# A two-layer GRU with a mixture of experts on one core: r's sums by a copy, ACT mixture work behind the tanh of n, a shorter preamble

## Chip, cores and metric

The kernel runs on one core of a Trainium2 chip, in fp32. The metric is the device time of one execution in microseconds (us). PE is the matrix engine, DVE the vector engine, ACT the scalar engine, POOL the GpSimd engine; SP issues the DMAs. Instructions of an engine run in the order of its program; engines wait for each other by semaphores.

## The reference, cut to what matters

```python
# x: [2, 1024, 256]; context: [2, 256]
mixed = tanh(x @ W_in.T + b_in + context)
h1 = gru(mixed, Wih0, Whh0, bih0, bhh0)
h2 = gru(h1, Wih1, Whh1, bih1, bhh1)
gate = sigmoid(context @ W_gate.T + b_gate)
x = x + (gate * h2 + h2) @ W_out.T + b_out
shared = silu(x @ w1) * (x @ w3) @ w2
s = sigmoid(concat(x, context) @ router_W)          # 8 experts, the best 2 by s + router_bias
routed = sum over experts e of combine[:, e] * (gelu(x @ W1e[e]) @ W2e[e])
out = x + (shared + routed) / 3

# one step of a GRU
r = sigmoid(xr + hr); z = sigmoid(xz + hz)          # x* = x @ Wih.T + bih, h* = h @ Whh.T + bhh
n = tanh(xn + r * hn)
h = (1 - z) * n + z * h
```

## The kernel before, in words

The two GRU layers run interleaved. A slot s holds step s of layer 0 and step s - LAG of layer 1 (`schedule`, L263); LAG is 20. There are 1024 steps, in chunks of CH = 16; j is the place in a layer-0 chunk, s % 16. Time steps and the two sequences of the batch lie along PSUM partitions: a chunk has 32 rows, four strips of 32 partitions hold four quarters of the 256 units.

PSUM holds, for each layer and each of two chunks in turn, `sums` (four parts of 64 columns: the state's part of n, then z, r, and the input's part of n) and `r_sums` (r alone). Ahead of a chunk they are filled with biases and with the product of the chunk's inputs and w_x. The input product is made in pieces on PE (`projection_pieces`, L52, `project_at`, L344): piece R (`project_r`, L308, 64 columns into `r_sums`) and pieces A, one for each half kt of the inputs (`project_all`, L313, 192 columns into `sums`). Layer 0's pieces stand at j = 8, 10 and 12 behind layer 1's products of the slot, layer 1's at j = 1, 2 and 3 ahead of them. Biases for the chunk after next come by two ACT copies, r's at a chunk's step 1 (L472), all at step 2 (L484).

A step of a layer, in the order of its dependences:

- PE: state times w_h for r (L330, 64 columns, into `r_sums`), then for n and z (L340, 128 columns). At j = 6 and 14 (`r_first`) one product of 192 columns makes all three, and r is turned later.
- DVE: r turned by 32x32 transposes (L402), then n (L411) and z (L412).
- ACT: tanh for r (L470) and for z (L478).
- DVE: a scan makes xn + r * hn (L420); ACT: tanh of n (L482); POOL: half the old state (L520).
- DVE: a scan makes the new state (L431).

At j = 13, and for layer 1 at j = 3, DVE turns the input's part of n of the next chunk (`turn_xn`, L387), layer 0's between the scan of n and the state scan, layer 1's behind the scan of n and so ahead of layer 0's turn of r and layer 1's state scan of the next slot (`dve_slots`, L434). POOL copies the chunk's inputs to `stage` at j = 0 (L525, L550), and SP clears the semaphores of the chunk before last.

Beside this runs the rest, for groups of 128 steps (256 rows), one group MLAG = BODY + LAG + 5 slots behind. The class `Mixture` (L64) makes its plan once: each operation gets a half slot (0: beside layer 0's step, 1: beside layer 1's), an engine does one a half slot, and `busy` (L92) names half slots that stay free. An ACT or DVE operation may stand in the same half slot as the PE product that it reads. A group has 94 products on PE, 83 operations on DVE and 22 on ACT: the tanh of 2 score halves (L656), the tanh of 4 shared units (L677), the gelu of 8 experts in 2 halves each (L688). In `act_slots` (L493) the first half slot's operation stands between layer 0's tanh of r and its tanh of z and n; the second one's between layer 1's tanh of r and of z and n.

The first product of the kernel, tanh(x @ W_in.T + ...), is made in blocks of TB = 512 rows. Ahead of the first slot PE makes the gate's products, the router's from the context, the first block, the biases of both layers in 128-row products against ones, and the first chunk's input product; the other blocks follow in pieces (`MIXING`) between slots 4 and 31.

The order within a slot on PE and the places of the ACT and DVE mixture work:

```python
recur(pe, 0, t0)                       # then MIXING piece, layer 1's input piece
mixture_at(pe, "pe", s, 0, base)
recur(pe, 1, t1)                       # then layer 0's input piece
```

## Time and profile before

| | |
|---|---|
| median of 3 runs | 2235.19 us (2231.73 to 2236.82) |
| profiled execution | 2234.58 us |
| its span (first to last instruction) | 2232.8 us |
| mean granted share of PE's clock | 0.995 |
| busy: PE, DVE, ACT, POOL | 94%, 82%, 53%, 24% |

In a row, "a<-b" is what is written and read by the program's names, "x16" the number of instructions merged (an fp32 product is two instructions; eight products of four strips are x16), and the bracket is the engine's idle time just before and what ended it. L431 is a line of the kernel. A busy PE means that a product is in flight, its fill included.

### The profile page before, as it was taken

The numbers are of one execution on the slowest core, as the hardware profiler recorded it, in microseconds if no ns is written. First come the engines' busy times: TensorE is split into PE (matmuls) and PEld (weight loads), VectorE is DVE, ScalarE is ACT, GpSimd is POOL, SyncE is SP. The second block draws the span as 40 slices with busy tenths as digits, with TensorE's granted clock in tenths as the row PEclk, the third lists the DMA queues.
The fourth block names the chain that finished last, engine by engine and source line by source line (L and its number), as shares of the span: only waits on it lengthen the run. The fifth ranks groups of instructions, "written<-read, shape, count | busy, mean of one in ns | idle before, by whom it ended". The sixth has DMA issues, their size and how long they took to land.

```text
span 2232.8 us, 165488 instructions
## 1 busy us (share of the span) xinstructions
PE 2095.5 (94%) x71788; PEld 1526.4 (68%) x71788; DVE 1835.4 (82%) x11070; ACT 1193.2 (53%) x6589; POOL 541.5 (24%) x2410
## 2 busy tenths in 40 slices
PE   6989899999999999999999999999999999999968
PEld 4666666677776776777767677777777677677744
DVE  4788888888888888888888888888888888888853
ACT  2555555555555555555555555555555555555531
POOL 1222222222222222222222222222222222222210
PEclk9999999999999999999999999999999999999998
DMA  5000000000000000000000000000000000000000
GB/s 214 4 5 5 5 5 5 23 5 5 10 5 24 5 5 9 5 24 5 5 10 24 5 5 10 5 24 5 5 10 5 24 5 5 9 5 24 5 8 26
DMA packets 7772, 32.98 MB, mean 15 GB/s; under 512 B 1328, under 2 KB 3456, under 8 KB 5760
## 3 DMA queue, kind: packets, MB, share of 16 engines
q1 hardware_dynamic: 7040, 22.38, 2.7%
q8 instruction: 562, 9.21, 1.6%
q14 instruction: 170, 1.39, 0.2%
HBM read 20.22 MB, written 2.16 MB: 10 GB/s over the span
## 4 chain that ended last, share of the span: by engine, by line
PE 56%; DVE 27%; ACT 13%; issue 3%; DMA 1%; SPq 0%; POOL 0%; DVEq 0%; POOLq 0%
PE bank L340 24%; PE bank L330 19%; PE bank L273 10%; DVE n_first L411 9%; DVE cells L431 8%; ACT factors L478 6%; ACT cells L482 5%; DVE r_pre L402 4%; DVE z_pre L412 3%; PE bank L313 3%; DVE bank L420 1%; PE bank L308 1%; ACT act_t L688 1%; ACT act_t L677 0%; PE bank L636 0%
## 5 line engine op out<-in xcount | busy, mean ns | idle before, releaser
L340 PE MATMUL bank<-w_h,cells 128*14 128x128 f32 (+4 forms) x32768 | 1362.7, 281 | 18.3 <-DVE cells L431 10.9
L340 PEld LDWEIGHTS bank<-w_h,cells 128*14 128x14 f32 (+4 forms) x32768 | 857.5, 110 | 118.5 <-DVE cells L431 85.1
L330 PEld LDWEIGHTS bank<-w_h,cells 128*14 128x14 f32 (+4 forms) x28672 | 533.1, 112 | 528.9 <-DVE cells L431 501.8
L330 PE MATMUL bank<-w_h,cells 128*14 128x64 f32 (+4 forms) x28672 | 787.4, 224 | 97.1 <-DVE cells L431 79.2
L520 POOL TENSOR_SCALAR cells<-cells 128x4 f32<-128x4 f32 x2048 | 463.6, 226 | 1615.4 <-DVE cells L431 1612.5
L470 ACT ACTIVATE n_second<-r_pre 128x4 f32<-128x4 f32 x2048 | 426.3, 208 | 538.3 <-DVE r_pre L402 509.9
L478 ACT ACTIVATE factors<-z_pre 128x4 f32<-128x4 f32 x2048 | 428.2, 209 | 403.6 <-DVE z_pre L412 345.0
L431 DVE TENSOR_TENSOR_SCAN cells<-factors,cells 128x18 f32<-128x18 f32 x2048 | 398.3, 194 | 277.0 <-ACT cells L482 203.7
L411 DVE STREAM_TRANSPOSE n_first<-bank 128x64 f32<-128x64 f32 x2048 | 597.2, 292 | 32.1 <-PE bank L340 23.9
L402 DVE STREAM_TRANSPOSE r_pre<-bank 128x64 f32<-128x64 f32 x2048 | 480.0, 234 | 29.6 <-PE bank L330 23.5
L412 DVE STREAM_TRANSPOSE z_pre<-bank 128x64 f32<-128x64 f32 x2048 | 427.3, 209 | 0.0
L420 DVE TENSOR_TENSOR_SCAN bank<-n_first,n_second 128x12 f32<-128x12 f32 x2048 | 394.4, 193 | 5.0
L482 ACT ACTIVATE cells<-bank 128x8 f32<-128x8 f32 x2048 | 366.6, 179 | 1.3
L273 PE MATMUL bank<-hid,w_2e 128*32 128x256 f32 x2048 | 157.8, 383 | 5.6 <-DVE hid L701 5.5
L273 PE MATMUL bank<-x,w_1e 128*32 128x256 f32 x2048 | 159.0, 381 | 0.1
L313 PE MATMUL bank<-w_x,stage 128*32 128x192 f32 x2048 | 135.5, 327 | 1.2 <-DVE z_pre L412 1.0
L701 DVE TENSOR_TENSOR hid<-act_t,c_all 128x128 f32<-128x128 f32 x256 | 68.7, 276 | 25.4 <-PE bank L273 12.7
L273 PE MATMUL bank<-x,w 128*32 128x256 f32 x1024 | 79.6, 386 | 0.0
L273 PEld LDWEIGHTS bank<-hid,w_2e 128*32 128x32 f32 x2048 | 65.7, 111 | 16.5 <-DVE hid L701 6.2
L688 ACT ACTIVATE act_t<-bank 128x256 f32<-128x256 f32 x128 | 47.3, 376 | 47.8 <-PE bank L273 47.8
L273 PEld LDWEIGHTS bank<-x,w_1e 128*32 128x32 f32 x2048 | 66.2, 111 | 9.6 <-issue 3.0
L313 PEld LDWEIGHTS bank<-w_x,stage 128*32 128x32 f32 x2048 | 65.1, 110 | 3.5 <-DVE z_pre L412 2.6
(89 smaller groups left out, 615.0 us busy)
## 6 DMA issues: line engine op xcount, KB each, us to landing
c_all<-weights SPq DMA_DIRECT2D x8, 1024.0 KB
x_t<-in_x_t SPq DMA_DIRECT2D x4, 512.0 KB, 6.6
w_1e<-in_w_1e SPq DMA_DIRECT2D x1, 2048.0 KB
w_2e<-in_w_2e SPq DMA_DIRECT2D x1, 2048.0 KB
out_y<-y SPq DMA_DIRECT2D x8, 256.0 KB, 2.7
w_x<-in_w_x SPq DMA_DIRECT2D x2, 768.0 KB, 7.8
w_h<-in_w_h SPq DMA_DIRECT2D x2, 768.0 KB, 9.3
w<-in_w SPq DMA_DIRECT2D x3, 512.0 KB
```

What stands on the lines that cost most here:

```text
L273: mm = pe.matmul(ps[strip], w[:, strip], x, start=start, stop=stop, tile_position=(0, 32 * g), skip_group_check=True)
L330: mm = pe.matmul(r_sums[l][p][32 * g:32 * g + B * (j + 1)], state_tile(l, j, kt), w_h[l][:, kt, g, 2 * U:], start=False, stop=False, tile_ ...
L340: mm = pe.matmul(sums[l][p][32 * g:32 * g + B * (j + 1), 0:width], state_tile(l, j, kt), w_h[l][:, kt, g, 0:width], start=False, stop=Fals ...
L402: v.transpose(r_pre[l][:].rearrange("p i b -> p b i"), blocks(at)).then_inc(s["turn"], 1)
L411: v.transpose(n_first[l][:, :, :, 2].rearrange("p i b -> p b i"), blocks(sums[l][p][:, 0:U])).then_inc(s["for_n"], 1)
L412: v.transpose(z_pre[l][:].rearrange("p i b -> p b i"), blocks(sums[l][p][:, U:2 * U])).then_inc(s["turn"], 1)
L420: v.tensor_tensor_scan(n_scan[l], n_first[l][:, own].rearrange("p i b e -> p (i b e)"), n_second[l][p][:, own].rearrange("p i b e -> p (i ...
L431: v.tensor_tensor_scan(step_cells(l, (j + 1) % CH, 0), factors[l][:, 2:], step_cells(l, j), 0.0, ALU.mult, ALU.add)\
L470: act.activation(n_second[l][p][:, own, :, 0], r_pre[l][:, own], ACT.Tanh, scale=0.5).then_inc(s["for_n"], 1)
L478: act.activation(cell_part(factors[l][:], 2), z_pre[l][:, own_rows(j)], ACT.Tanh, scale=0.5)
L482: act.activation(to, n.to_broadcast([P, B, UB, 2]), ACT.Tanh).then_inc(s["for_h"], 1)
L520: pool.tensor_scalar(cell_part(step_rows(l, j), 3), cell_part(step_rows(l, j), 1), 0.5, None, ALU.mult)\
```

## The change

Eight things. LAG is 19. The R pieces go: the A pieces write r into `sums` alone, and `take_x`, in place of `turn_xn`, has DVE copy it from there into `r_sums` ahead of the turn of n; for layer 1 this stands at j = 2, its A pieces at j = 1 and 2. The ACT copy of r's biases (L472) goes with them. In `act_slots` the mixture's operation stands behind layer 0's tanh of n, ahead of layer 1's tanh of r, and the planner gives ACT first half slots alone. The planner's free half slots follow. Ahead of the first slot only 64 rows of x and layer 0's biases are worked on; the rest of the first block, layer 1's biases and the gate's products move into slots 0 to 10. Bias products have two rows instead of 128, and no area has to be zeroed. Loads are issued in another order.

```diff
-LAG = CH + 4
+LAG = CH + 3
...
+FIRST = 2 * ROWS
...
-    return {8: (R, None), 10: (A, 0), 12: (A, 1)} if l == 0 else {1: (R, None), 2: (A, 0), 3: (A, 1)}
+    return {10: 0, 12: 1} if l == 0 else {1: 0, 2: 1}
...
-    free = [s for s in range(1, BODY) if s % CH > 3]
-    pieces = [(i, q, kt) for i in range(KT, KT * B * T // TB) for q in range(2) for kt in range(KT)]
+    free = [s for s in range(3, BODY) if s < LAG or s % CH == 0 or s % CH > 2]
+    pieces = [(i, q, kt) for i in range(KT * B * T // TB) for q in range(2) for kt in range(KT)]
...
-            return ((j - LAG) if part else j) % CH in (1, 2)
-        return (j, part) in ((13, 0), (3, 1))
+            return part == 1 or j == 2
+        return (j, part) in ((13, 0), (2, 1))
...
-        first_loads = [(w_in, "w_in"), (b_in, "b_in"), (cond, "cond"), (w_gate, "w_gate"), (b_gate, "b_gate"), (w_r, "w_r")]
+        first_loads = [(w_in, "w_in"), (b_in, "b_in"), (cond, "cond")]
+        gate_loads = [(w_gate, "w_gate"), (b_gate, "b_gate"), (w_r, "w_r")]
...
+                if i == 2:
+                    pe.wait_ge(s_gate, KT + 1)
...
+        def bias_rows(pe, ps, l, g, gate, width, start):
+
+            return pe.matmul(ps[32 * g:32 * g + 32], ones[0:2, :], w_b[l][0:2, g, gate * U:(gate + width) * U], start=start, stop=False,
+                             tile_position=(0, 32 * g), skip_group_check=True)
 
         def place_biases(pe, l):
 
             for p in range(2):
                 for g in range(NQ):
-                    strip = slice(32 * g, 32 * g + 32)
-                    pe.matmul(sums[l][p][strip], ones[:, :], w_b[l][:, g, :], start=p == 0, stop=False,
-                              tile_position=(0, 32 * g), skip_group_check=True)
-                    mm = pe.matmul(r_sums[l][p][strip], ones[:, :], w_b[l][:, g, 2 * U:3 * U], start=p == 0, stop=False,
-                                   tile_position=(0, 32 * g), skip_group_check=True)
-            mm.then_inc(s_bps, 1)
-
-        def project_r(pe, l, p):
+                    bias_rows(pe, sums[l][p], l, g, 0, NGATE, p == 0)
+                    mm = bias_rows(pe, r_sums[l][p], l, g, 2, 1, p == 0)
+            return mm
+
+        def gate_products(pe):
+
+            pe.wait_ge(s_gld, 16 * len(gate_loads))
+            pe.wait_ge(s_bsb, 1)
+            for m in range(KT):
+                for kt in range(KT):
+                    pe.matmul(banks[6][:, B * m:B * m + B], feature_tile(w_gate[:, kt], m), cond[:, kt, :],
+                              start=(m == kt == 0), stop=(kt == KT - 1), skip_group_check=True)
             for kt in range(KT):
-                for g in range(NQ):
-                    pe.matmul(r_sums[l][p][32 * g:32 * g + 32], stage[l][:, kt, :], w_x[l][:, kt, g, U:2 * U],
-                              start=False, stop=False, tile_position=(0, 32 * g), skip_group_check=True)
+                mm = pe.matmul(banks[6][0:E, B * KT:B * KT + B], w_r[:, KT + kt, :], cond[:, kt, :], start=False, stop=(kt == KT - 1),
+                               skip_group_check=True)
+            mm.then_inc(s_cps, 1)
...
+            if j == 0:
+                pe.wait_ge(sets[l][1 - p]["xn"], 1)
...
-            piece, kt = projection_pieces(l)[s % CH]
+            kt = projection_pieces(l)[s % CH]
             p = s // CH % 2
             t = s if l == 0 else s - 1 - LAG
-            if piece == R:
+            if kt == 0:
                 pe.wait_ge(sets[0][p]["pool"], staged)
                 if l == 1 and s // CH == 1:
                     pe.wait_ge(s_wld[1], 16 * len(gru_loads[1]))
                 if t >= CH:
-                    pe.wait_ge(sets[l][p]["bias"], 2)
-                if t >= 0:
-                    pe.wait_ge(sets[l][p]["turn"], 2 * (t % CH) + 1)
-                project_r(pe, l, 1 - p)
-            else:
-                if t >= 0:
-                    pe.wait_ge(sets[l][p]["turn"], 2 * (t % CH) + 2)
-                mm = project_all(pe, l, 1 - p, kt)
-                if kt == KT - 1:
-                    mm.then_inc(sets[l][p]["x"], 1)
+                    pe.wait_ge(sets[l][p]["bias"], 1)
+            if t >= 0:
+                pe.wait_ge(sets[l][p]["turn"], 2 * (t % CH) + 2)
+            mm = project_all(pe, l, 1 - p, kt)
+            if kt == KT - 1:
+                mm.then_inc(sets[l][p]["x"], 1)
...
+                if s == 0:
+                    for g in range(NQ):
+                        mm = bias_rows(pe, banks[6][:, 0:NGATE * U], 0, g, 0, NGATE, True)
+                    mm.then_inc(s_bps, 1)
+                if s == 1:
+                    place_biases(pe, 1).then_inc(s_bps, 1)
+                if s == 2:
+                    gate_products(pe)
...
-        def turn_xn(v, l, p):
-
+        def take_x(v, l, p):
+
...
-                        turn_xn(v, 0, 1 - p)
+                        take_x(v, 0, 1 - p)
                 mixture_at(v, "dve", s, 0, base)
+                if s == 1:
+                    v.wait_ge(s_bps, 1)
+                    v.tensor_copy(biases[0][:], banks[6][:, 0:NGATE * U]).then_inc(s_bsb, 1)
+                if s == 2:
+                    v.wait_ge(s_bps, 2)
+                    v.tensor_copy(biases[1][:], sums[1][0]).then_inc(s_bsb, 1)
+                    v.wait_ge(s_gld, 16 * len(gate_loads))
+                    v.tensor_scalar(b_gate_half[:], b_gate[:], 0.5, None, ALU.mult).then_inc(s_bias, 1)
+                if s == 4:
+                    v.wait_ge(s_gate, KT + 1)
+                    v.tensor_scalar(gate1[:], gate_th[:], 0.5, 1.5, ALU.mult, ALU.add).then_inc(s_bias, 1)
                 if t0 is not None:
                     dve_h(v, 0, t0)
                 if t1 is not None:
                     dve_turn_r(v, 1, t1)
                     dve_turn_nz(v, 1, t1)
                     dve_n(v, 1, t1)
-                if CH <= s < T + CH and j == 3:
+                if CH <= s < T + CH and j == 2:
                     v.wait_ge(sets[1][p]["x"], 1)
-                    turn_xn(v, 1, 1 - p)
+                    take_x(v, 1, 1 - p)
...
-            if j == 1 and places_biases(t):
-                act.activation(r_sums[l][1 - p], biases[l][:, 2 * U:3 * U], ACT.Identity).then_inc(s["bias"], 1)
...
-        def mixed_tanh(act, i, b):
+        def mixed_tanh(act, i, b, first=False):
             nb, m = divmod(i, KT)
             if b == 0:
-                act.wait_ge(s_mps, i + 1)
-            act.activation(mixed[:, m, nb * TB + b:(nb + 1) * TB:B], banks[4 + i % 3][:, b::B], ACT.Tanh,
+                act.wait_ge(s_mps, i + 1 + (0 if first else KT))
+            begin, end = (0, FIRST) if first else (FIRST if i < KT else 0, TB)
+            act.activation(mixed[:, m, nb * TB + begin + b:nb * TB + end:B], banks[4 + i % 3][:, begin + b:end:B], ACT.Tanh,
                            bias=in_bias[:, m, b:b + 1]).then_inc(s_mix, 1)
+
+        def gate_tanh(act):
+            act.wait_ge(s_bias, 2)
+            act.wait_ge(s_cps, 1)
+            for m in range(KT):
+                act.activation(gate_th[:, m, :], banks[6][:, B * m:B * m + B], ACT.Tanh, bias=b_gate_half[:, m:m + 1], scale=0.5)\
+                   .then_inc(s_gate, 1)
+            act.activation(r_bias[:], banks[6][0:E, B * KT:B * KT + B], ACT.Identity, scale=0.5).then_inc(s_gate, 1)
 
         def act_slots(act, s0, n, base):
             for s, t0, t1 in schedule(s0, n):
                 done = MIXING[s - 1][0] if s - 1 in MIXING and MIXING[s - 1][1:] == (1, KT - 1) else None
+                if s == 3:
+                    gate_tanh(act)
                 if t0 is not None:
                     act_r(act, 0, t0)
+                if t0 is not None:
+                    act_zn(act, 0, t0)
                 if done is not None:
                     mixed_tanh(act, done, 0)
                 mixture_at(act, "act", s, 0, base)
-                if t0 is not None:
-                    act_zn(act, 0, t0)
                 if t1 is not None:
                     act_r(act, 1, t1)
+                    act_zn(act, 1, t1)
                 if done is not None:
                     mixed_tanh(act, done, 1)
                 mixture_at(act, "act", s, 1, base)
-                if t1 is not None:
-                    act_zn(act, 1, t1)
...
-                        if c % (TB // ROWS) == TB // ROWS - 1 and c < T // CH - 1:
-                            pool.wait_ge(s_mix, B * KT * ((c + 1) * ROWS // TB + 1))
+                        if c == 1 or c % (TB // ROWS) == TB // ROWS - 1 and c < T // CH - 1:
+                            pool.wait_ge(s_mix, B * KT * ((c + 1) * ROWS // TB + 2))
...
+            sp.dma_start(w_in[:], a["w_in"]).then_inc(s_ld, 16)
+            sp.dma_start(x_t[:, :, 0:FIRST], a["x_t"][:, :, 0:FIRST]).then_inc(s_x1ld, 16)
+            for t, name in first_loads[1:]:
                 sp.dma_start(t[:], a[name]).then_inc(s_ld, 16)
-            load_x(sp, 0)
             for t, name in gru_loads[0]:
                 sp.dma_start(t[:], a[name]).then_inc(s_wld[0], 16)
-            sp.wait_ge(s_set, 2)
             for l in range(2):
-                sp.dma_start(w_b[l][0:1, :, U:NGATE * U], a[f"b_x{l}"]).then_inc(s_bld, 16)
-                sp.dma_start(w_b[l][1:2, :, 0:3 * U], a[f"b_h{l}"]).then_inc(s_bld, 16)
+                sp.dma_start(w_b[l][0:2], a[f"w_b{l}"]).then_inc(s_bld, 16)
+            for t, name in gate_loads:
+                sp.dma_start(t[:], a[name]).then_inc(s_gld, 16)
+            sp.dma_start(x_t[:, :, FIRST:TB], a["x_t"][:, :, FIRST:TB]).then_inc(s_xld[0], 16)
...
-            for m in range(KT):
+            pe.wait_ge(s_x1ld, 16)
+            for i in range(KT):
                 for kt in range(KT):
-                    pe.matmul(banks[0][:, B * m:B * m + B], feature_tile(w_gate[:, kt], m), cond[:, kt, :],
-                              start=(kt == 0), stop=(kt == KT - 1))
-            for kt in range(KT):
-                mm = pe.matmul(banks[1][0:E, 0:B], w_r[:, KT + kt, :], cond[:, kt, :], start=(kt == 0), stop=(kt == KT - 1))
-            mm.then_inc(s_cps, 1)
-            for i in range(KT):
-                for q in range(2):
-                    for kt in range(KT):
-                        mix_input(pe, i, q, kt)
-            pe.wait_ge(s_bld, 16 * 4)
-            pe.wait_ge(s_gate, KT + 1)
-            for l in range(2):
-                place_biases(pe, l)
-            pe.wait_ge(s_bsb, 1)
+                    mix_input(pe, i, None, kt)
+            pe.wait_ge(s_bld, 16 * 2)
+            pe.wait_ge(s_set, 1)
+            place_biases(pe, 0)
             pe.wait_ge(s_wld[0], 16 * len(gru_loads[0]))
             pe.wait_ge(s_stg, 1)
-            project_r(pe, 0, 0)
...
-            v.wait_ge(s_gate, KT + 1)
-            v.tensor_scalar(gate1[:], gate_th[:], 0.5, 1.5, ALU.mult, ALU.add).then_inc(s_bias, 1)
-            for l in range(2):
-                v.wait_ge(s_bps, l + 1)
-                v.tensor_copy(biases[l][:], sums[l][0]).then_inc(s_bsb, 1)
             v.wait_ge(s_x0, 1)
-            turn_xn(v, 0, 0)
+            take_x(v, 0, 0)
```

## Rows read from the trace of the kernel before

**Rows 1.** The page, parts 1 and 4: busy time, and the chain by engine and line.

```profile
PE 2095.5 (94%) x71788; PEld 1526.4 (68%) x71788; DVE 1835.4 (82%) x11070; ACT 1193.2 (53%) x6589; POOL 541.5 (24%) x2410
...
PE 56%; DVE 27%; ACT 13%; issue 3%; DMA 1%; SPq 0%; POOL 0%; DVEq 0%; POOLq 0%
PE bank L340 24%; PE bank L330 19%; PE bank L273 10%; DVE n_first L411 9%; DVE cells L431 8%; ACT factors L478 6%; ACT cells L482 5%; DVE r_pre L402 4%; DVE z_pre L412 3%; PE bank L313 3%; DVE bank L420 1%; PE bank L308 1%; ACT act_t L688 1%; ACT act_t L677 0%; PE bank L636 0%
```

**Rows 2.** Windows of the state scans alone (x is their number).

```profile
150.00:325.00 175.00, 34.03 (x174) 1.00 0.02 5
400.00:600.00 200.00, 37.64 (x194) 1.00 0.04 11
```

**Rows 3.** Timeline (start, length, instruction): a slot without ACT mixture work.

```profile
1191.60 0.20 DVE L431 TENSOR_TENSOR_SCAN cells<-factors,cells 128x18 f32<-128x18 f32 x1
...
1191.88 0.41 PE L330 MATMUL bank<-w_h,cells 128*10 128x64 f32 x16
...
1192.47 0.20 DVE L431 TENSOR_TENSOR_SCAN cells<-factors,cells 128x18 f32<-128x18 f32 x1 [0.25 <-ACT cells L482]
...
1193.58 0.20 DVE L431 TENSOR_TENSOR_SCAN cells<-factors,cells 128x18 f32<-128x18 f32 x1
```

**Rows 4.** Timeline: the score's slot, and the slot of a shared expert's tanh.

```profile
1149.21 0.20 DVE L431 TENSOR_TENSOR_SCAN cells<-factors,cells 128x18 f32<-128x18 f32 x1
...
1151.71 0.20 DVE L431 TENSOR_TENSOR_SCAN cells<-factors,cells 128x18 f32<-128x18 f32 x1
...
1157.75 0.20 DVE L431 TENSOR_TENSOR_SCAN cells<-factors,cells 128x18 f32<-128x18 f32 x1
...
1158.28 0.38 ACT L677 ACTIVATE act_t<-bank 128x256 f32<-128x256 f32 x1 [0.38 <-PE bank L273]
...
1159.92 0.18 DVE L431 TENSOR_TENSOR_SCAN cells<-factors,cells 128x18 f32<-128x18 f32 x1
```

**Rows 5.** Timeline: ACT behind layer 0's tanh of n at j = 2.

```profile
188.41 0.38 ACT L484 ACTIVATE bank<-biases 128x256 f32<-128x256 f32 x1
...
188.92 0.21 ACT L470 ACTIVATE n_second<-r_pre 128x4 f32<-128x4 f32 x1
```

**Rows 6.** Timeline: the products of r at j = 8, and layer 0's next.

```profile
1192.54 0.41 PE L308 MATMUL bank<-w_x,stage 128*32 128x64 f32 x16
...
1192.76 0.41 PE L330 MATMUL bank<-w_h,cells 128*20 128x64 f32 x16
```

**Rows 7.** Timeline: DVE at j = 3; and L875 by its source line.

```profile
191.42 0.19 DVE L420 TENSOR_TENSOR_SCAN bank<-n_first,n_second 128x12 f32<-128x12 f32 x1
...
191.52 0.28 DVE L387 STREAM_TRANSPOSE n_second<-bank 128x64 f32<-128x64 f32 x1
...
191.67 0.21 DVE L402 STREAM_TRANSPOSE r_pre<-bank 128x64 f32<-128x64 f32 x1
191.85 0.20 DVE L431 TENSOR_TENSOR_SCAN cells<-factors,cells 128x18 f32<-128x18 f32 x1
...
L875 DVE COPY biases<-bank x2: 424/424/424, 15.6 to 16.7; 128x256 f32<-128x256 f32 x2
```

**Rows 8.** Start: issue and landing (last column, us) of w_h0, and the first state.

```profile
4.91 0.43 SPq L803 DMA_DIRECT2D w_h<-in_w_h  x1
...
w_h<-in_w_h SPq DMA_DIRECT2D x1, 768.0 KB, 7.9
...
19.39 0.20 DVE L431 TENSOR_TENSOR_SCAN cells<-factors,cells 128x18 f32<-128x18 f32 x1 [0.31 <-ACT cells L482]
```

**Rows 9.** A window of the start (PEclk third from last), and a step in it.

```profile
24.00:28.00 4.00, 2.92 (x72) 1.66 (x72) 1.77 (x10) 1.05 (x6) 0.40 (x2) 0.76 1.02 430
...
25.60 0.20 DVE L431 TENSOR_TENSOR_SCAN cells<-factors,cells 128x18 f32<-128x18 f32 x1 [0.24 <-ACT cells L482]
...
27.97 0.19 DVE L431 TENSOR_TENSOR_SCAN cells<-factors,cells 128x18 f32<-128x18 f32 x1 [0.24 <-ACT cells L482]
```

**Rows 10.** Timeline: PE in a step of layer 1 alone.

```profile
2168.45 0.46 PE L330 MATMUL bank<-w_h,cells 128*30 128x64 f32 x16 [1.09 <-DVE cells L431]
```

44 lines of the change are left out of this document (19 added, 25 removed).

## The prediction

> **What bounds the kernel now.** I read the page first. PE is busy for 94% of the span, yet the chain that ended last is PE for only 56% and DVE and ACT for 40% [rows 1]: no engine is the limit alone. The limit is a loop. A step of one layer needs PE (products from the state), DVE (three transposes, two scans) and ACT (three tanh), and the two layers take turns. I call the stretch in which each layer makes one step a slot; step s is the slot's number, j its place in a chunk of 16.
>
> Second, windows over the state scan (L431, two per slot). Between 150 and 325 us, where no mixture work runs, 174 scans fit in 175 us: 2.01 us a slot. Between 400 and 600 us, with the mixture, 194 fit in 200 us: 2.06 us [rows 2]. The mixture costs 0.05 us in each of about 870 slots, some 44 us, and the question is which of its work costs that.
>
> Third, single slots in the timeline. In a slot without ACT mixture work, 1.98 us pass from layer 1's state to its next (1191.60 to 1193.58), layer 0's in between at 1192.47 [rows 3]. In a slot with one, the shared expert's tanh (L677, 0.38 us) stands ahead of layer 0's tanh of z and n. It waits 0.38 us for a PE product, starts at 1158.28, and the slot takes 1157.75 to 1159.92 = 2.17 us. The slot of the router's scores takes 1149.21 to 1151.71 = 2.50 us [rows 4].
>
> **1. Mixture on ACT behind the tanh of n.** The planner, followed, gives each group of 128 slots 22 ACT operations: 15 in the first half of a slot, 7 in the second. Thirteen of the 15 stand in the very slot of the last product that they read. One of these (first half of expert 0) falls on j = 6, where r is turned late and ACT is ahead anyway: none counted. One is the score: 2.50 - 1.98 = 0.52. Eleven cost 2.17 - 1.98 = 0.19 each. That is 11 x 0.19 + 0.52 = 2.6 us a group; seven groups run beside the recurrences: 18.2 us. In the new place all 22 stand between layer 0's tanh of n and layer 1's tanh of r. The bias copy L484 already stands exactly there at j = 2: it starts at 188.41, lasts 0.38 us, and the tanh of r starts at 188.92 [rows 5], so 0.51 us are free for an operation of 0.38. The product it waits for is over by 1158.28, and the tanh of n, some 0.2 us ahead of a state scan due at 1157.75 + 0.87, starts near 1158.4. New cost 0, **gain 18.2 us**; bounds 0 (the wait moves to the tanh of r) and 20.
>
> **2. No separate products of r.** L308 disappears: 127 pieces (one at the start), each holding PE for 0.22 us (1192.54 to the next product at 1192.76) [rows 6]. That is 28 us of PE time, the upper bound; the chain gives L308 1%, some 22 us [rows 1]. But layer 0's next product begins 0.29 us behind the state scan of 1192.47 with a piece in front of it, and 0.28 behind the scan of 1191.60 without one [rows 3, 6]: PE had to wait for the state anyway. Between 0 and 22 I stay near the timeline and take a tenth of the chain's share: **gain 2.2 us**. The waits that it carried (staged rows, biases, turned z) move to the first full piece, long met. The ACT copy of r's biases (124 of 0.21 us) stood between tanh of r and of z, where ACT waits for DVE: taken as 0, bounds 0 and 26.
>
> **3. DVE copies r (take_x).** 128 copies of 128x64 out of PSUM. No row shows one. The nearest: L875 copies 256 columns in 0.42 us, and a transpose of 64 columns lasts 0.21. I take 0.21, and of it 0.10 on DVE's path: L387 starts 0.10 behind a scan of 0.19 us, and the 0.28 us long L387 is followed after 0.15, so successors start 0.09 to 0.13 before an operation's end [rows 7]. Layer 0 (j = 13): between the scan of n and the state scan 0.43 us pass, waiting for ACT; copy at +0.10, L387 at +0.20, both out of the way at about +0.37: 0. Layer 1 (now j = 2): the turn of layer 0's r is queued behind it as well and the state scan stands behind all three: +0.10, 63 times: **cost 6.3 us**. Bounds 0 and 128 x 0.21 = 27. The Trainium skill speaks against this part: VectorE: DVE Perf Modes, section The DRAIN you can't avoid, says that the next operation does not start until the pipe is empty. By it every copy would cost its whole length, 27 us, and the total would be 2239 (milder than rival B below). The rows of L387 show overlap instead, so I keep the 0.10.
>
> **4. LAG 19.** One slot of layer 1 alone less, and everything behind it a slot earlier: **gain 2.0 us** (1.98, as in [rows 3]). The planner now avoids two j instead of three on PE and ends a group in 116 slots instead of 127: the same operations in fewer slots, 0. Staged rows for layer 1 have one slot less time; POOL copies them at j = 0 within about 0.5 us: 0.
>
> **5. The start.** The first state comes at 19.39. PE must have w_h0, issued at 4.9, landed 7.9 us later at 12.8 [rows 8]. Ahead of it 0.25 MB of w_gate and 0.45 MB of x no longer stand, and three issues (about 1.5 us): at the 430 GB/s that the row of [rows 9] shows it lands at 10 to 11 us. Then follow bias products of one layer only, both products of kt, take_x, the first step. Before, 6.6 us lay between landing and state, of which waits for the mixing were part; PE will have been idle before and slower now, so I keep about 5.5: first state near 16.2, 3.2 earlier. The moved work (bias rows, layer 1's biases, gate products, two DVE copies of 0.42 [rows 7], the gate's tanh) comes back in slots 0 to 4, where only layer 0 runs and PE stands idle for about 1.1 us of each, as for a lone layer 1 [rows 10]; some overflows: -1.2. The waits of SP and POOL at s = 0 are not later. Net **gain 2.0 us**, bounds 0 and 5.
>
> **6. A thinner end.** The second last group now finishes in slot 1034, so the last nine slots have layer 1's products alone, PE idle 1.09 us of each [rows 10]. Such slots stood at the start: there the granted clock fell (0.76 over 24 to 28 us), and a step took 25.60 to 27.97 = 2.37 us [rows 9], 0.39 over 1.98. Nine steps at the lower level (1.2 GHz) would cost 0.39 x 9 = 3.5; **cost 2.0**, bounds 0 and 5 (the output group then starts slow too). The Trainium skill, TensorE: Matmul & The Clock Gate, section Terms, prices time at the lower level at half of it: 9 us for the 18 us of these nine steps, and the total would be 2225.5. The step in [rows 9] lost 16%, since DVE and ACT don't slow down.
>
> **Sum.** -18.2 - 2.2 + 6.3 - 2.0 - 2.0 + 2.0 = -16.1. The profiled execution took 2234.6 (span 2232.8), so 2218.5. It lies 0.6 under the median of the runs, 2235.2, well within their spread.
>
> **Rivals.**
> A. The new place is not free: the mixture operation holds layer 1's tanh of r as it held layer 0's tanh of z. For it: there are 22 there instead of 15, each with one or two waits. Against: 0.51 us of room, shown by L484 124 times at both layers together. The 18.2 fall away: 2236.7, no change.
> B. Slower: take_x blocks DVE. Place: between scan of n and state scan, in both layers; if the copy doesn't overlap and its wait for PE costs something too, 0.3 us each. 127 x 0.3 = 38 instead of 6.3: 2250. It decides from (16.1 + 6.3)/127 = 0.18 us a copy. Against: L387 costs nothing visible in the same place.
> C. Better: take_x hides wholly, since the half slot behind it has slack on DVE, and the clock holds at the end: 2210.
> D. It does not do what it says at the start: bias products wait for w_b, which is now queued behind w_h0, with PE at its lower level through slots 0 to 6: start worth 0 and end costs 5: 2223.
>
> **How the numbers follow.** About 0.2%, 4.5 us, is what a measurement of this kernel can tell from no change. Forecast 0.63, A 0.08, B 0.07, C 0.13, D 0.09. The predicted time is the forecast's. C and D fix the range at first; with the bounds of take_x and of the ACT term it runs from 2208 to 2230, leaving out B and most of A. Faster: forecast, C, D and a little of A, 0.86; same 0.07; slower 0.07.
>
> **What would show it.** Right: windows between 400 and 1400 us with 195 or 196 state scans in 200 us; L688, L677 and L656 with hardly any idle time released by PE in front of them; L470 of layer 1 still at about 0.5 us behind tanh of n in those slots; the first L431 near 16; a copy of 128x64 of about 0.2 us, with the state scan 0.43 behind the scan of n at j = 13 and 0.53 at j = 2. Wrong: idle time of DVE ahead of the scan of n (L420) released by ACT in mixture slots (A), state scans 0.7 behind the scan of n at the copies (B), or a granted clock below 1.00 for more than about 10 us around the end (D).

## The result, and the profile after

The changed kernel takes **2225.13 us** (median of 6 runs, 2223.01 to 2229.72); the kernel before took 2236.79 beside it (6 runs, 2231.73 to 2240.54). The ratio is 0.9949, interval 0.9934 to 0.9964: faster by 11.7 us. The forecast was 16.1 less than the profiled execution of before, or 18.3 less than the median beside it. The sign and the range held, and the main mechanism, that of ACT. Of the sizes several did not, one effect stood in no term, and the start came out right by another path than the one that I had read. The profiled execution was the slowest of the six: 2229.7 us, span 2227.9, so against the profiled one of before (2234.6) it is only 4.9 better. In what follows, slot places are read over many slots, and whole times from medians.

First the page of the changed kernel: its busy times and the chain that ended last, by engine and line. L347 are now the products of r, L355 those of n and z (L330 and L340 before), L451 the state scan, L511 the tanh of n.

```profile
PE 2092.4 (94%) x69780; PEld 1486.6 (67%) x69780; DVE 1839.0 (83%) x11196; ACT 1198.2 (54%) x6469; POOL 545.0 (24%) x2410
...
PE 51%; DVE 32%; ACT 13%; issue 3%; DMA 1%; SPq 0%; POOL 0%; DVEq 0%; POOLq 0%
```

Against [rows 1], 2008 products and as many loads of weights are gone, but PE is 3.1 us less busy, not 28. The products that stay did not grow: a product of 192 columns of the inputs lasts 327 ns before and 328 after. A busy PE is time with any product in flight, and the pieces lay beside others. DVE has 126 instructions more, and its share of the chain goes from 27% to 32%.

Windows over the state scan (DVE busy, number of scans in brackets, granted clock), the changed kernel:

```profile
150.00:325.00 175.00, 33.42 (x172) 1.00 0.02 5
400.00:600.00 200.00, 37.49 (x195) 1.00 0.04 11
600.00:800.00 200.00, 37.25 (x194) 1.00 0.03 10
1000.00:1200.00 200.00, 37.73 (x196) 1.00 0.02 6
```

Against [rows 2], from 400 to 600 us 195 scans stand where 194 stood, but 172 where 174 stood, in the stretch without mixture work beside it. The recurrence itself did not become shorter. To see where, I took from the trace the time from the end of each state scan of layer 1 to the end of its next, for slots 160 to 1019, and the median of each place j in the chunk (53 or 54 slots each):

```
j        0     1     2     3     4     5     6     7     8     9     10    11    12    13    14    15    sum
before  1.983 1.984 1.996 2.013 2.007 1.940 2.142 1.976 1.974 2.019 2.022 2.072 1.989 2.073 2.157 2.037  32.384
after   1.992 2.000 2.053 2.006 1.942 1.971 2.250 1.954 1.966 1.971 1.971 2.072 1.983 2.076 2.157 2.042  32.406
```

Sixteen slots take as long as before. j = 4, 9 and 10 became shorter by 0.05 to 0.07 each; j = 2 became longer by 0.06 and **j = 6 by 0.11**. These medians repeat on other chips within about 0.01, except where PE stalls (below), so they can carry an experiment with a single execution.

**j = 6.** Timeline of the changed kernel (start, length, instruction, idle time before it):

```profile
192.84 0.38 ACT L513 ACTIVATE bank<-biases 128x256 f32<-128x256 f32 x1
192.98 0.20 DVE L451 TENSOR_TENSOR_SCAN cells<-factors,cells 128x18 f32<-128x18 f32 x1 [0.25 <-ACT cells L511]
...
193.37 0.84 PE L355 MATMUL bank<-w_h,cells 128*8 128x192 f32 x16 [0.35 <-ACT bank L513]
...
194.06 0.20 DVE L451 TENSOR_TENSOR_SCAN cells<-factors,cells 128x18 f32<-128x18 f32 x1 [0.25 <-ACT cells L511]
```

L513 is ACT's copy of layer 1's biases (L484 before). In both kernels it runs right behind layer 1's own tanh of n, but in the changed one the products that wait for it are now those of a step in which r, n and z come in one product of 192 columns. They start at 193.37, 0.39 behind the state scan of 192.98. The same place in the kernel before:

```profile
197.79 0.38 ACT L484 ACTIVATE bank<-biases 128x256 f32<-128x256 f32 x1
197.93 0.20 DVE L431 TENSOR_TENSOR_SCAN cells<-factors,cells 128x18 f32<-128x18 f32 x1
...
198.18 0.42 PE L330 MATMUL bank<-w_h,cells 128*8 128x64 f32 x16 [0.20 <-DVE cells L431]
...
198.41 0.62 PE L340 MATMUL bank<-w_h,cells 128*8 128x128 f32 x16
198.82 0.20 DVE L431 TENSOR_TENSOR_SCAN cells<-factors,cells 128x18 f32<-128x18 f32 x1 [0.25 <-ACT cells L482]
```

There the products of r (L330) go into another bank and start 0.25 behind the scan. The bias copy, for which only L340 waits, is over meanwhile.

**j = 2, take_x.** DVE of the changed kernel around layer 1's copy of r (L406):

```profile
186.49 0.19 DVE L440 TENSOR_TENSOR_SCAN bank<-n_first,n_second 128x12 f32<-128x12 f32 x1
186.59 0.21 DVE L406 COPY bank<-bank 128x64 f32<-128x64 f32 x1
186.71 0.28 DVE L407 STREAM_TRANSPOSE n_second<-bank 128x64 f32<-128x64 f32 x1
186.88 0.20 DVE L422 STREAM_TRANSPOSE r_pre<-bank 128x64 f32<-128x64 f32 x1
187.01 0.15 DVE L451 TENSOR_TENSOR_SCAN cells<-factors,cells 128x18 f32<-128x18 f32 x1
```

The copy lasts 0.21, and L407 starts 0.12 behind the copy's start, as L387 let its successor start early in [rows 7]. The state scan is 0.52 behind the scan of n (0.53 forecast at j = 2); at j = 13 it is 0.44 (0.43 forecast).

**ACT.** A slot with expert work of ACT, and the slot of the router's scores:

```profile
1316.35 0.20 DVE L451 TENSOR_TENSOR_SCAN cells<-factors,cells 128x18 f32<-128x18 f32 x1
...
1317.08 0.38 ACT L728 ACTIVATE act_t<-bank 128x256 f32<-128x256 f32 x1
...
1318.33 0.18 DVE L451 TENSOR_TENSOR_SCAN cells<-factors,cells 128x18 f32<-128x18 f32 x1
```

```profile
607.73 0.81 PE L676 MATMUL bank<-x,w_r 128*8 128x256 f32 x3
...
607.92 0.20 DVE L451 TENSOR_TENSOR_SCAN cells<-factors,cells 128x18 f32<-128x18 f32 x1
...
608.59 0.34 PE L347 MATMUL bank<-w_h,cells 128*28 128x64 f32 x9
...
608.79 0.38 ACT L696 ACTIVATE score_th<-bank,r_bias 8x128 f32<-8x128 f32 x1
...
610.28 0.20 DVE L451 TENSOR_TENSOR_SCAN cells<-factors,cells 128x18 f32<-128x18 f32 x1
```

The first takes 1.98 us, as if the ACT work were not there, where such a slot took 2.17 [rows 4]. The second takes 2.36, where it took 2.50: of its excess only 0.14 went. ACT (L696) isn't what it waits for; both router products (L676) stand on PE ahead of layer 1's products of r (L347), most of which come at 608.59, 0.67 behind the scan of 607.92.

**Start.** The first state scan starts at 16.27 in place of 19.39 [rows 8], 3.1 earlier, and at the end of layer 0's 41st state 1.9 us are left (101.18 against 103.06). But it was not w_h0 that held it. In the kernel before, w_h0 landed at 12.8 and its first products began later, behind the products of the first block, of the biases and of the inputs:

```profile
17.23 0.48 PE L330 MATMUL bank<-w_h,cells 128*2 128x64 f32 x16
```

In the changed kernel w_h0 landed at 9.6. PE waited for the rows of the biases (w_b) until 9.54, made their products, then those of the inputs, and began those of the state behind take_x:

```profile
9.54 2.38 PE L302 MATMUL bank<-hist,ones 2*32 2x256 f32 x32 [4.04 <-DMA hist<-in_w_b]
...
13.91 0.61 PE L347 MATMUL bank<-w_h,cells 128*2 128x64 f32 x16 [0.55 <-DVE n_second L407]
```

The lead of 3.1 us is gone four steps later: the fifth state scan starts at 28.38, where it started at 27.97 before [rows 9]. The work that moved into slots 0 to 2 stands on the chain there, biases and gate (start, length):

```profile
17.99 2.30 PE bank L302 x32
...
21.69 1.80 PE bank L319 x8
```

The 1.9 us were won again afterwards, in slots in which the kernel before was slow: slots 5 and 18, where its granted clock was at 0.50 for a while (2.56 and 2.55 us against 1.95 and 1.94), and slot 26, where PE stalled (3.06 against 1.98).

**End.** At the end layer 1 runs alone. Windows there (PE, PEld, DVE, ACT, POOL, then the granted clock, third from last):

```profile
2140.00:2150.00 10.00, 5.82 (x176) 3.77 (x176) 5.39 (x28) 2.52 (x15) 1.14 (x5) 0.89 0.09 29
2150.00:2160.00 10.00, 6.01 (x112) 3.50 (x112) 3.36 (x18) 1.97 (x12) 0.91 (x4) 0.50 0.01 2
2160.00:2170.00 10.00, 3.83 (x72) 2.51 (x76) 2.58 (x14) 1.37 (x8) 3.26 (x8) 0.50 0.01 2
```

A clock of 0.50 is the lower of the two levels, 1.2 GHz. From 2130 to 2140 PE had been busy for 6.4 of 10 us. The scans in it:

```profile
2150.15 0.20 DVE L451 TENSOR_TENSOR_SCAN cells<-factors,cells 128x18 f32<-128x18 f32 x1 [0.25 <-ACT cells L511]
2152.73 0.20 DVE L451 TENSOR_TENSOR_SCAN cells<-factors,cells 128x18 f32<-128x18 f32 x1 [0.24 <-ACT cells L511]
```

2.58 us a step instead of 1.95 to 1.96 in the steps ahead of the fall. From slot 1019 to the last state the kernel before took 47.8 us, so 45.8 with a slot less; the changed one took 50.2. The seven slow steps thus cost 4.4 us.

### The profile page after: what moved, and what is told of

The parts are those of the page before. It is cut to its first block, busy times and chain, and to the rows that moved or that the text cites. A ratio compares the mean times of both kernels' runs of the same rounds, so it can differ in the third digit from the quotient of the medians.

```text
span 2227.9 us, 161674 instructions
## 1 busy us (share of the span) xinstructions
PE 2092.4 (94%) x69780; PEld 1486.6 (67%) x69780; DVE 1839.0 (83%) x11196; ACT 1198.2 (54%) x6469; POOL 545.0 (24%) x2410
## 4 chain that ended last, share of the span: by engine, by line
PE 51%; DVE 32%; ACT 13%; issue 3%; DMA 1%; SPq 0%; POOL 0%; DVEq 0%; POOLq 0%
PE bank L355 23%; PE bank L347 17%; DVE n_first L431 11%; PE bank L274 9%; DVE cells L451 8%; ACT factors L507 7%; ACT cells L511 5%; DVE r_pre L422 5%; DVE z_pre L432 4%; PE bank L328 3%; DVE bank L440 2%; DVE n_second L407 1%; DVE bank L406 0%; DVE x L690 0%; PE bank L676 0%
## 5 line engine op out<-in xcount | busy, mean ns | idle before, releaser
L355 PE MATMUL bank<-w_h,cells 128*22 128x128 f32 (+4 forms) x32768 | 1360.6, 281 | 18.4 <-DVE cells L451 6.9
L355 PEld LDWEIGHTS bank<-w_h,cells 128*22 128x22 f32 (+4 forms) x32768 | 858.4, 111 | 118.2 <-DVE cells L451 91.2
L347 PEld LDWEIGHTS bank<-w_h,cells 128*22 128x22 f32 (+4 forms) x28672 | 529.6, 112 | 560.4 <-DVE cells L451 539.7
L347 PE MATMUL bank<-w_h,cells 128*22 128x64 f32 (+4 forms) x28672 | 785.4, 225 | 92.0 <-DVE cells L451 70.5
L451 DVE TENSOR_TENSOR_SCAN cells<-factors,cells 128x18 f32<-128x18 f32 x2048 | 395.4, 193 | 258.4 <-ACT cells L511 191.9
L511 ACT ACTIVATE cells<-bank 128x8 f32<-128x8 f32 x2048 | 369.2, 180 | 1.5 <-DVE bank L440 0.2
L741 DVE TENSOR_TENSOR hid<-act_t,c_all 128x128 f32<-128x128 f32 x256 | 68.7, 276 | 25.8 <-PE bank L274 18.8
L728 ACT ACTIVATE act_t<-bank 128x256 f32<-128x256 f32 x128 | 47.7, 379 | 30.7 <-PE bank L274 30.6
```

Source lines behind the costliest of these rows:

```text
L347: mm = pe.matmul(r_sums[l][p][32 * g:32 * g + B * (j + 1)], state_tile(l, j, kt), w_h[l][:, kt, g, 2 * U:], start=False, stop=False, tile_ ...
L355: mm = pe.matmul(sums[l][p][32 * g:32 * g + B * (j + 1), 0:width], state_tile(l, j, kt), w_h[l][:, kt, g, 0:width], start=False, stop=Fals ...
L451: v.tensor_tensor_scan(step_cells(l, (j + 1) % CH, 0), factors[l][:, 2:], step_cells(l, j), 0.0, ALU.mult, ALU.add)\
L511: act.activation(to, n.to_broadcast([P, B, UB, 2]), ACT.Tanh).then_inc(s["for_h"], 1)
```

## The experiments

Twelve runs follow, nine of edited kernels and three of the kernels before and after, on three other chips. The chips are slower: the kernel before takes 2267.1, 2270.7 and 2268.8 us there, where it takes 2236.8 on the first, at the same granted clock. So each kernel is judged by its ratio to the kernel before on its own chip, and differences are taken within a chip. What the first chip's ratio of 0.9949 is elsewhere: the changed kernel again gave 0.9932 (0.9910 to 0.9955) and 0.9926 (0.9901 to 0.9951), which is 18.8 and 16.2 us.

**The bias copy of layer 1 a step earlier:** the first pair of lines is PE's wait for it, the second ACT's copy.

```diff
-            if j == 3 and places_biases(t):
+            if j == 3 - l and places_biases(t):
...
-            if j == 2 and places_biases(t):
+            if j == 2 - l and places_biases(t):
```

> The changed kernel, with layer 1's bias copy on ACT at its step 1 instead of 2, and PE's wait for it at step 2 instead of 3. Theory: with LAG 19 layer 1's step without separate r products (j = 6) is also the one in which PE waits for the bias copy, so nothing covers the wait; it costs 0.12 us in 62 chunks. Then the slot at j = 6 falls from 2.25 to about 2.13 us, and the time by 7 us, to about 2218 (0.992 of the kernel before). Rival: the two wide products of 192 columns in one slot collide whatever PE waits for; then j = 6 stays at 2.25 and the time at 2225 (0.995).

Measured: 2243.91 us (6 runs), 0.9899 (0.9875 to 0.9923). j = 6 fell to 2.125, j = 3 rose to 2.038, j = 5 was 1.959 and j = 7 1.975. Summed over the 16 places 32.313 against 32.406, so 0.093 x 54 = 5.0 us of net gain. The rise at j = 3 did not come again with the same edit in the last kernel below (2.010). The place in the trace:

```profile
193.65 0.20 DVE L451 TENSOR_TENSOR_SCAN cells<-factors,cells 128x18 f32<-128x18 f32 x1 [0.24 <-ACT cells L511]
...
193.90 0.84 PE L355 MATMUL bank<-w_h,cells 128*8 128x192 f32 x16 [0.21 <-DVE cells L451]
```

The products now start 0.25 behind the scan and wait for nothing but it. The missed term is shown, and the rival of that run, two wide products that collide whatever PE waits for, is refuted.

**LAG back at 20.**

```diff
-LAG = CH + 3
+LAG = CH + 4
```

> The changed kernel with LAG back at 20, nothing else. Theory of the uncovered bias wait: j = 6 at 2.13 instead of 2.25 us (7 us gained), one slot more (2 us lost): about 2220, so LAG 19 alone was a loss of 5 us. Rival (LAG 19 is worth its slot, the loss at j = 6 has another cause): about 2227, j = 6 at 2.25.

Measured: 2242.67 us (5 runs), 0.9887 (0.9861 to 0.9913), level with the run above on the same chip. j = 6 is 2.139, as before the change, but j = 4 is 2.005 again, not 1.942. LAG sets which place of layer 1 meets which place of layer 0. It gained 0.06 at one j and lost 0.11 at another, 54 times each; its slot less at the end is all that a reading of the last slots sees. By these numbers LAG 19 alone is worth about nothing: 5.8 - 3.5 - 2.0 = 0.3 us lost. In whole times the ratio with LAG 20 is 0.004 to 0.005 under those of the changed kernel, some 9 us, but these stem from other chips; what the rest of it is was not shown.

**The ACT part alone,** put into the kernel before: layer 0's tanh of z and n ahead of the mixture's first half, layer 1's ahead of its second, and the planner gives ACT first half slots alone.

```diff
+                if t0 is not None:
+                    act_zn(act, 0, t0)
...
-                if t0 is not None:
-                    act_zn(act, 0, t0)
```

> The kernel before with the mixture's ACT work behind the tanh of n alone (and the planner giving ACT first half slots only). Theory: eleven operations a group save 0.19 us each; the score's slot saves only 0.13, since layer 1's products wait behind both router products on PE; 2.2 us in each of seven groups: 15.6 us, so 2221 (0.993). Rival 1, the prediction's sum: 18.2 us, 2218.5 (0.992). Rival 2, part of the stall moves to the other layer's steps: 8 us or less, 2229 (0.9965).

Measured: 2261.01 us (12 runs), 0.9973 (0.9958 to 0.9989): 6.1 us, not 15.6. Yet its slots with ACT work lie on the medians of their places, but for stalls: j = 12 stands at 2.092 and j = 10 at 2.147 (1.989 and 2.022 in the first trace of before), and 84 us of idle time are put down to issue, over all engines, against 77 in the kernel before on another of the slower chips. That pointed to a cost that comes with the place of the instructions, not with their work; the 9 us between the slots and the total are not accounted for otherwise.

**The changed kernel with ACT's old places** (the reverse edit).

> The changed kernel with the mixture's ACT work back in its old places. Theory: 15.6 us slower than the changed kernel, 2241 (1.002 of the kernel before): without this part the change would be a loss. Rival (the gain comes from the r pieces and the start, and the ACT part is worth 8 us or less): 2233 or less (0.998).

Measured: 2256.89 us (10 runs), 0.9953 (0.9935 to 0.9971). The score's slot is 2.54, 0.18 longer than in the changed kernel, and two more slots of each group at j = 0 are 0.19 longer. The changed kernel itself did not run on this chip. Against the kernel with the early bias copy it is 13.0 slower; less the 5.0 of that copy, some 8 us are left for ACT's places. The slots bear this out. The plan that comes with LAG 19 puts the 13 first half operations of ACT elsewhere than the plan of before, six of them at j = 6 and 14 and one at j = 10, where the old place costs nothing. Six others, slots 0, 32, 64, 84, 92 and 120 of a group, are 0.15 to 0.20 longer than in the changed kernel (of each place the second shortest of its six or seven slots, so as to leave stalls out): 1.1 us a group, 7.9 over seven. In the plan of before it was 11 x 0.19 + 0.13 = 2.2 us a group, 15.5 over seven. So about half of the 15.5 us comes with the new plan alone, and the other half with the new place behind the tanh of n.

**The end filled:** a product of no use in each of the last eight slots.

```diff
+                if T + 10 < s < T + LAG:
+                    by_columns(pe, ups[0][:, 0], feature_tile(w_out[:, 0], 0), hist[:, 0, 0:TG], True, True)
```

> The changed kernel with one product of 256 columns without use beside each of the last eight steps of layer 1, where PE's pieces have run out. Theory: the granted clock stays at its upper level until the last step; those steps take 1.97 instead of 2.6 us, 5 us in all, and the output group begins at the upper level, up to 1 us more: 6 us below the changed kernel in its profile. Where the changed kernel's clock happened not to fall, nothing. Rival (the long steps have another cause, or the fillers delay them): no gain.

Measured: 2244.88 us (4 runs), 0.9904 (0.9878 to 0.9929), 7.0 under the changed kernel beside it (2251.89); the intervals of the two ratios overlap. In its trace the clock stays at 1.00 to 2190, and the twelve last steps take 1.95 to 2.15 us. From slot 1019 to the last state it needs 46.0 us, the changed kernel 50.2, 47.7 and 49.3 in three executions: the clock falls at a different step in each, so the traces show 1.7 to 4.2 of the 7.0. The rest was not shown; stalls can move a time by as much.

**The instruction stream shifted:** 32 products of no use ahead of the steps, 64 matmuls and 64 loads of weights on PE; nothing else is changed.

```diff
+            for _ in range(32):
+                pe.matmul(banks[7][:, 0:16], w_in[:, 0, 0:P], x_t[:, 0, 0:16], start=True, stop=True)
```

> The changed kernel with 32 small products (128 PE instructions, 8 KB of code, no effect on any result) ahead of layer 0's bias products, where PE waits for its loads anyway. Theory: PE stalls at fixed points of its instruction stream, once a block of code comes too late; the points move against the steps, the same stalls fall on other slots, and the time changes by 2 to 10 us in either direction although the work is the same. Rival (stalls are random in time): no change beyond 0.2%, stalls in other slots in every run.

Measured: 2270.23 us (10 runs), 1.0002 (0.9982 to 1.0022), 18.3 above the changed kernel beside it. Of that 9.4 us is the products' own time (first state at 26.04 against 16.66), and the other 9 arise among steps that are the same, instruction for instruction: from slot 160 to 1019 it takes 1801.2 us against 1792.4, at the same granted clock, while the idle time put down to issue rises from 62 to 76 us. The medians of the places agree within 0.015 but one, j = 12: 2.108 against 1.989.

Single slots show that the place in the stream decides. Slot 67 of a group of 128 takes 2.22 to 2.26 us in six of seven groups of the changed kernel, and 2.15 to 2.25 in the same kernel on two other chips; its median place takes 2.01. With the stream shifted it takes 2.00 to 2.01 in all seven, and other slots are long instead. Of the slots in which PE or its loads stalled for over 0.25 us, 64 and 54 in the two executions of the changed kernel on the slower chips, 20 are the same (4 would be by chance); with the stream shifted 7 and 4 of 77 fall on them (6 and 5 would be by chance). The rival, stalls that are random in time, does not fit.

What such a stall is, three times one group of 128 slots apart, in the changed kernel on the third of these chips:

```profile
675.85 0.78 PEld L355 LDWEIGHTS bank<-w_h,cells 128*22 128x22 f32 x25 [0.39 <-issue]
...
940.02 0.82 PEld L355 LDWEIGHTS bank<-w_h,cells 128*22 128x22 f32 x26 [0.39 <-issue]
...
1206.71 1.13 PE L355 MATMUL bank<-w_h,cells 128*22 128x128 f32 x26 [0.40 <-issue]
```

PE stops in the middle of a run of products that wait for no semaphore; the slots take 2.52, 2.52 and 2.79 in place of 2.08. Waits put down to issue, the largest row each: the kernel before on the first chip, the changed one there, then both on a slower one (us in total, times, longest; the 4.6 is one wait, at 2169.2, behind the last state):

```profile
PEld bank L340 <- issue: 13.4, 35, 1.0
```

```profile
PEld bank L274 <- issue: 10.8, 28, 4.6
```

```profile
PEld bank L340 <- issue: 34.6, 84, 0.9
```

```profile
PEld bank L355 <- issue: 20.4, 53, 0.8
```

Added over all such rows it is 36 and 40 us on the first chip, 77 and 62 on the slower one. So the slower chip stalls more: the span of the kernel before is 39.0 us longer there, and these rows grow by 41. Between the two kernels they differ by 4 us more on the first chip and 15 less on the slower one, one execution each, so part of what the change gains is not in any slot's work. That the instructions' arrival is what fails is my reading: the queue that carries instructions has these rows, in the kernel before and in the changed one (packets, MB, share of the queues' time), but that each stall waits for one of its packets was not shown.

```profile
q8 instruction: 562, 9.21, 1.6%
```

```profile
q8 instruction: 547, 8.96, 1.6%
```

**The router's products in two slots:** the planner no longer puts the second beside the first.

```diff
-            mix.add("pe", f"route{kt}", ("x211",), product(ups[1][0:E, 0], w_r[:, kt], x2[:, kt], kt == 0, kt == KT - 1), beside=kt > 0)
+            mix.add("pe", f"route{kt}", ("x211",), product(ups[1][0:E, 0], w_r[:, kt], x2[:, kt], kt == 0, kt == KT - 1))
```

> The changed kernel with the two router products in two slots. If layer 1's r products wait behind both router products (0.85 us of PE in one slot), the router's slot falls from 2.36 to 2.05 to 2.15 us, one slot of each of 7 groups, and the slot that takes the second stays within 0.05 of its median. Rival: ACT's work or the accumulation bank makes the excess: the slot stays at 2.3 to 2.4.

Measured: 2252.88 us, one run, beside 2252.61 for the changed kernel. The score's slot is gone from the list of long ones:

```profile
613.98 0.20 DVE L451 TENSOR_TENSOR_SCAN cells<-factors,cells 128x18 f32<-128x18 f32 x1
...
614.23 0.46 PE L347 MATMUL bank<-w_h,cells 128*28 128x64 f32 x16
...
615.97 0.20 DVE L451 TENSOR_TENSOR_SCAN cells<-factors,cells 128x18 f32<-128x18 f32 x1
```

1.99 us, better than expected: the whole 0.37 that was left was the wait behind two router products, and none of it the score's. The 2.6 us that seven such slots give don't appear in the total; in this one execution stalls can have eaten them (78 us of issue against 65).

**The copy of r twice,** once into columns that nothing reads.

```diff
+            v.tensor_copy(banks[l][:, (4 + p) * U:(5 + p) * U], sums[l][p][:, 2 * U:3 * U])
             v.tensor_copy(r_sums[l][p], sums[l][p][:, 2 * U:3 * U])
```

> The changed kernel with VectorE's copy of r issued twice, once into a part of the bank that nothing reads. If the copy costs what its issue interval is (0.12 to 0.13 us) and only where VectorE's order of work is the bound: the third slot of the pattern rises from 2.05 to 2.15 to 2.18, the fourteenth (layer 0) from 2.07 to at most 2.10, some 8 us in all. Rival 1: a copy holds VectorE for its whole 0.21 us at either layer: both slots rise by 0.2, 26 us. Rival 2: the 0.057 us of the third slot came from PE, not from the copy: it stays at 2.05.

Measured: 2265.34 us, one run, 12.7 over the changed kernel's median on its chip. j = 2 rose from 2.052 to 2.185, 0.133, that is 8.4 us over 63 chunks. Layer 0's places rose little: j = 13 by 0.014, j = 14 by 0.024. The issue interval is the price at layer 1, as expected; rival 1 would have shown 0.2 at both. So the first copy, at 0.057 x 63 = 3.6 us, was half hidden, and a second finds no slack left. That the whole 0.057 is the copy's was not tried by itself: with LAG 20 it is 0.030 at j = 2 and 0.013 at j = 3.

**All three repairs together:** early bias copy, filled end, split router products.

> The changed kernel with three edits: ACT's bias copy issued a step earlier, as in e1_bias_early; a product of no use in each of the slots after layer 0's last step, as in e5_end_filled; and the two router products in two slots instead of one. If the three causes are separate and of the sizes read so far (0.12 x 62 = 7.4 us at layer 1's fourth step of a tile; 2 to 4 us in the stretch after layer 0's last step, which falls to about 46 us; 0.25 to 0.37 x 7 = 2 to 2.6 us at the router), it is 11 to 14 us below c2_after, a ratio to the kernel before of 0.987. Rival: each added or moved instruction of PE shifts all later ones against the fixed blocks in which the instruction stream comes, and what a repair gains is lost or won again by where the stalls fall: 0 to 8 us below c2_after, with the medians of steps 6 of the pattern at 2.13 all the same.

> The changed kernel itself, on the chip of e9_best, as its base. 0.993 to 0.995 of the kernel before by what was measured so far; the fourth step of a tile at 2.25, the router's slot at 2.36.

Measured: **2233.22 us** (5 runs, 2229.59 to 2238.53), ratio to the kernel before 0.9844 (0.9821 to 0.9867); the changed kernel beside it 2252.61. That is 19.4 us less than the change, and 35.6 less than before. In the trace: j = 6 at 2.129 and the pattern's sum 32.343 against 32.569; no score slot over 2.03; 46.0 us from slot 1019 to the last state against 49.3; issue 53 us against 65. The last windows, to be held against those above:

```profile
2140.00:2150.00 10.00, 6.52 (x196) 3.93 (x188) 4.84 (x26) 2.71 (x15) 1.14 (x5) 1.00 0.01 4
2150.00:2160.00 10.00, 6.95 (x200) 4.29 (x196) 5.53 (x29) 2.72 (x15) 1.14 (x5) 1.00 0.08 28
2160.00:2170.00 10.00, 4.14 (x126) 2.46 (x116) 3.65 (x19) 2.12 (x12) 3.40 (x9) 0.91 0.01 2
```

The causes read separately add to about 5.0 + 3.3 + 2.6 = 11; the other 8 or so fit stalls that fell better (issue 53 us, not 65; j = 12 at 2.020, not 2.116), which nobody planned and the next edit can undo. That the total is 19.4 and not 11 is luck.

The two base runs, for the record:

> The kernel before, unchanged, profiled on the same chip as the three kernels beside it. Both theories: medians of the slots by j as in its first profile within 0.01 us. If waits for PE instructions differ by chip, the total of PE's idle time put down to issue moves away from the 34 us of its first profile, and the time with it.

2273.9 us, its places as in the first trace within 0.01 except j = 10 (2.164 for 2.022), j = 11 (2.120 for 2.072) and j = 12 (2.170 for 1.989).

> The changed kernel, unchanged, as control. Theory: 0.995 of the kernel before on this chip too, slot at j = 6 2.25 us, idle time put down to issue as much above that of the kernel before as in the first pair (38 against 34 us). Rival (the ACT part is worth its 15 us and the first pair hid it by chance): 0.992 or less.

2251.89 us (5 runs). j = 2, 4 and 6 at 2.054, 1.939 and 2.250: the three shifts of the change repeat within 0.005.

## Why the prediction was right, and where its sizes were off

- **1, ACT (-18.2).** Mechanism right: ordinary ACT work costs 0 in its new place, and its waits moved to where ACT is idle anyway. Half of the gain did not need the new place, since the plan with LAG 19 had already put seven of the 13 operations where the old one costs nothing. The score was mis-sized. I priced its slot as 2.50 - 1.98 and gave all of it to ACT, though PE's two router products stood in the same slot; 0.14 of the 0.52 was ACT's, and 0.38 x 7 = 2.7 us stayed. By slots the term is 15.5. In whole times it showed 6.1 alone on a stalling chip; what it is on the first chip was not tried by itself. There slots 160 to 1019 became only 6.8 us shorter in the trace. New excess came in at fixed slots of each group, 61, 67, 69, 82 and 101, which are 0.16 to 0.45 longer than their medians and also long on two other chips; all but 61 lie on their medians again once the stream is shifted. The sign that I named for it was poor: L728 still has 31 us of idle time released by PE ahead of it (48 for L688 before), which harms nothing where it now lies.
- **2, pieces of r (-2.2).** Of its own it shows nothing: the kernel with the ACT part alone still has them, and its j = 7, 8 and 9 are 1.974, 1.968, 1.981, against 1.975, 1.966, 1.976 with LAG 20 and no pieces. Of the 0.05 at j = 9, 0.04 belongs to the ACT part by the same runs.
- **3, take_x (+6.3).** The mechanism held to 0.01 us: issue interval 0.12, state scan 0.52 behind the scan of n. The price was 3.6, over half of the 0.10 that I gave it. In the profile the copy's successor starts 0.09 before the copy's end. The Trainium skill, VectorE: DVE Perf Modes, section The DRAIN you can't avoid, has the next operation start only behind the emptied pipe, and the same section adds that one which is not held starts earlier, which I left out when I priced the copies by it at 27 us. The trace agrees with the exception and not with the rule: 0.12 to the successor, and 0.133 for a second copy, in place of 0.21.
- **4, LAG (-2.0).** The slot less is there. The step that failed is that I took a change of lag as the last slot only. It also moved layer 1's step with the wait for its biases onto the kind of step whose first product needs them: +0.11 at j = 6, 5.8 us over 54 chunks, against -0.065 at j = 4, 3.5 us. This is the part of the change that the prediction did not see at all, and undoing the wait gave 5.0.
- **5, start (-2.0).** -1.9, and the first state 3.1 earlier where I said 3.2: both numbers are luck. I took w_h0 for what the first step waits for. PE reached its products 4.4 us after it had landed before, and 4.3 after it, and what ended PE's long wait in the changed kernel was w_b. The moved work cost 3.5 us in slots 1 to 4 and not 1.2, since PE has it ahead of the products of the next step there; 2.3 came back where the kernel before had its slow slots 5, 18 and 26.
- **6, end (+2.0).** In the profiled execution 4.4, near the upper bound of 5, over seven steps and not nine. I scaled the step of [rows 9], 0.39 slower in a window at 0.76; at 0.50 it is 0.62, which makes the step 32% longer. The state scan lasts 0.20 us there as elsewhere, so DVE keeps its speed. In other executions the fall comes later and costs less. The Trainium skill, TensorE: Matmul & The Clock Gate, section Terms, prices time at the lower level at half of it, which would be 9.1 of the 18.3 us of these seven steps; the trace has 4.4, so pricing a step of three engines by it overstates.

Together: 2.7 (score) + 5.8 - 3.5 (lag) + 2.2 (pieces) + 2.4 (end) - 2.7 (take_x) = 6.9 less gain than forecast, 9.2 in place of 16.1; 11.7 were measured in medians, 4.9 between the two profiles, and stalls of some microseconds either way lie between. That the total came as near as it did is in part luck: errors of 2 to 6 us stand on both sides of the sum. Of the rivals, A and B are refuted by the timelines. C failed on both counts, as the copy costs something and the clock fell. D fits at the end, and at the start in that PE waited for w_b, though the start kept 1.9 us.

## What to carry to other kernels

When two recurrences are interleaved, a change of their lag is a change of every pairing of steps: list for each step with a special wait which step of the other layer it will meet, and whether its first product is the one that waits. Work that moves into slots with an idle engine is free only if it stands behind the chain's next product there, and not ahead of it. Before giving a long slot to one engine, look at what else stands in that slot; two causes that coincide hide one another. And in a long unrolled program, an edit worth under 1% should be judged by medians of repeated places beside the total, for the total also holds where the stalls happen to fall.

## What the runs showed of the hardware that I had not expected

- PE stalls in the midst of products without a wait. In one execution of the kernel before on a slower chip 178 such waits of over 0.15 us stand between 110 and 2100 us, 131 of them under 0.5. They come at the same places of repeating code, and in part at the same places on two chips. 64 more matmuls, with 64 loads, ahead of the loop moved them and made the unchanged rest 9 us of 1792 longer. Their sum differs between chips: 36 us of issue idle time on one, 77 on another, for the same kernel, at a granted clock of 0.99 and over. It goes with a kernel that is 1.5% slower there.
- The lower clock at a thin end comes at a different step in each execution of one kernel: 18.3, 7.5 and 14.9 us ahead of the last state in three traces. A product of no use in each of the last eight slots kept it away and was repaid in medians.
